# An LSTM decoder on one core: the doubled cell in a PSUM bank, the half cell behind h, and a new spread of two PE jobs

## The chip, the core and the metric

The kernel runs on one core of a Trainium2 chip. Time is device time in microseconds (us) of one launch on that core; smaller is better. The core's engines are TensorE (PE, with its weight loads as PEld), VectorE (DVE), ScalarE (ACT), GpSimd (POOL) and SyncE (SP). They run their own instruction streams and meet through semaphores. PE writes PSUM (eight banks of 128 partitions); DVE and ACT read and write both PSUM and SBUF.

## What is computed

Sixteen sequences of 1024 tokens with 64 features go through three layers with residuals. The second layer is an LSTM autoencoder: two encoder LSTMs (forward, backward) of 1024 steps, then a decoder LSTM of 1024 steps whose input is the same at every step, then a projection. The third is a mixture of 8 experts with the two best chosen per token.

```python
def step(carry, xw):
    h, c = carry
    z = xw + h @ U
    i, f, g, o = jnp.split(z, 4, axis=-1)
    i = jax.nn.sigmoid(i)
    f = jax.nn.sigmoid(f)
    g = jnp.tanh(g)
    o = jax.nn.sigmoid(o)
    c = f * c + i * g
    h = o * jnp.tanh(c)
    return ((h, c), h)
...
h = _L0_tok_ref(x, ...)
h = h + _L0_attn_ref(_layernorm(h, axis=-1), ...)
h = h + _L0_ffn_ref(_layernorm(h, axis=-1), ...)
```

## The kernel before, in words

The program has four parts, one after the other: a set-up, the token mixing, the encoder (both directions interleaved, 1024 steps each), and the decoder, which carries the experts' work in its gaps. The change touches the decoder alone.

**One decoder step.** State lies as 128 hidden units by 16 sequences. PE (`pe_gates`, L733 to 746) multiplies h by U. h is held as two f16 parts, so there are twelve small matmuls: eight on the high part (L740, low then high weights), four on the low part (L743). ACT (`act_gates`) takes the tanh of the gates i, f, g (L751, 48 columns) and of o (L753); the sigmoids are made from tanh of half the argument. DVE (`dve_terms`, L766) makes both products, `dve_sum` (L772) adds them to `twice_cell`, twice the new cell. ACT (`act_cell`, L758) writes tanh of half of that to `tanh_cell`, the first 16 columns of PSUM bank 3. DVE makes the output gate (L789) and the half of twice_cell, the cell that the next step's terms read (`dve_half_cell`, L783), then h: its high part (L797), its full f32 value (L798), and the low part (L803), which waits for L798's semaphore. With the high and the low part PE starts the next step.

DVE's own stream in a step, written in `body` of its block (before, L1349 to 1359): terms, sum, output gate, half cell, the `in_tanh` pieces of the experts' work, then h high, h, h low, then the `in_gates` pieces. All engines work their streams in the order written.

**Bodies and places.** The 1024 steps are 32 bodies of 32 steps (`BODY`). A place is the number of a step in its body, 0 to 31. From body 1 on, each body also carries the experts' work on a tile of 512 tokens: place s carries the tile's part s, and part s + 32 of the tile before. PE's stream at a place is: the twelve gate matmuls, the refill of the input term (`fill`, L1044) at the places that are 1, 3 or 5 in their group of eight, the parts (`pe_part`), then unread products (`pe_idle`, L731: an identity times a constant tile into a spare part of a bank, read by nobody), and at places 7, 15, 23 and 31 one more refill. Their number per place is `idle_products(step, tiles)`: 10 or 13 at places 3 to 18, a small table elsewhere, 5 at place 19.

**The transposes of the experts' sums.** Parts 37 and 38, which fall on places 5 and 6 of the next body, turn the 64 x 512 f32 result `yT` (made by ACT in part 36) in four matmuls (L1129) of one block each, two in each part; the trace records each as two f32 passes. DVE adds them to the residual in part 43, place 11 (L1307). The refill at place 5 stands ahead of them.

So at place s, PE's parts and unread products stand between the gates of step s and the gates of step s + 1. If they take too long, it is h of step s that finds PE busy, and h of step s + 1 that comes late.

Of the kernel before, what the change touches and what calls it, by code (L numbers as in the profile page):

```python
# [6 lines left out]
F32, F16, BF16 = mybir.dt.float32, mybir.dt.float16, mybir.dt.bfloat16  # L7
ALU = mybir.AluOpType
ACT = mybir.ActivationFunctionType
AX = mybir.AxisListType  # L10

P = 128
B, T, D = 16, 1024, 64
# [46 lines left out]
class Links:  # L60


    def __init__(self, engine, sem, base=0):
        self.engine, self.sem, self.base, self.n = engine, sem, base, 0
# [637 lines left out]
class Chain:  # L702
# [3 lines left out]

    def __init__(self, sb, sem, d, name, cell_bank):
        self.d = d  # L710
        self.tanh_cell = cell_bank[:, 0:B]
        self.ifg_cell = sb(f"ifg_cell_{name}", [P, 4, B], F32)
        self.terms = sb(f"terms_{name}", [P, 2, B], F32)
        self.twice_cell, self.tanh_o, self.out_gate, self.h = (
            sb(f"{part}_{name}", [P, B], F32) for part in ("twice_cell", "tanh_o", "out_gate", "h"))
        (self.s_z_ifg, self.s_z_o, self.s_t_ifg, self.s_t_o, self.s_terms, self.s_out_gate, self.s_twice,
         self.s_cell, self.s_tanh_cell, self.s_hi, self.s_h, self.s_lo) = (sem(f"{s}_{name}") for s in (
             "z_ifg", "z_o", "t_ifg", "t_o", "terms", "out_gate", "twice", "cell", "tanh_cell", "hi", "h", "lo"))

    def start(self, nc, own):  # L720

        own.link(nc.vector.memset(self.twice_cell[:], 0.0))
        nc.vector.memset(self.ifg_cell[:, 3, :], 0.0).then_inc(self.s_cell, 1)


# [29 lines left out]

def act_cell(nc, act, c, n):
    act.wait_ge(c.s_twice, n + 1)
    nc.scalar.activation(c.tanh_cell, c.twice_cell[:], ACT.Tanh, scale=0.5).then_inc(c.s_tanh_cell, 1)  # L758


def dve_terms(nc, dve, c, n, own_cell=True):
# [7 lines left out]

def dve_sum(nc, dve, c, n):  # L770
    dve.wait_ge(c.s_terms, n + 1)
    nc.vector.tensor_tensor(c.twice_cell[:], c.terms[:, 0, :], c.terms[:, 1, :], ALU.add).then_inc(c.s_twice, 1)  # L772


def act_out_gate(nc, act, c, n, half_scale):
# [4 lines left out]

def dve_half_cell(nc, dve, c, sums):
    dve.wait_ge(c.s_twice, sums)
    nc.vector.tensor_scalar(c.ifg_cell[:, 3, :], c.twice_cell[:], 0.5, None, ALU.mult).then_inc(c.s_cell, 1)  # L783


def dve_rest(nc, dve, c, n, sums):

    dve.wait_ge(c.s_t_o, n + 1)
    nc.vector.tensor_scalar(c.out_gate[:], c.tanh_o[:], 1.0, 0.5 * X_SCALE, ALU.add, ALU.mult  # L789
                            ).then_inc(c.s_out_gate, 1)  # L790
    dve_half_cell(nc, dve, c, sums)


def dve_hidden(nc, dve, c, n, h_hi):

    tt = nc.vector.tensor_tensor
    tt(h_hi, c.out_gate[:], c.tanh_cell, ALU.mult).then_inc(c.s_hi, 1)  # L797
    tt(c.h[:], c.out_gate[:], c.tanh_cell, ALU.mult).then_inc(c.s_h, 1)  # L798


def dve_hidden_low(nc, dve, c, n, h_hi, h_lo):
    dve.wait_ge(c.s_h, n + 1)
    nc.vector.tensor_tensor(h_lo, c.h[:], h_hi, ALU.subtract).then_inc(c.s_lo, 1)  # L803
# [108 lines left out]
def idle_products(step, tiles):  # L912

    if not tiles or 3 <= step < 19:
        return 10 if step % 2 else 13
    by_place = {0: 0, 1: 4, 2: 5, 19: 5, 20: 9}
    return by_place.get(step, 4 if step % 2 == 0 else 6 if step % STEPS == STEPS - 1 else 5)


QS = BODY * B // P  # L920
# [4 lines left out]
def decoder_and_experts(nc, m):  # L925
# [5 lines left out]

    ctx, sb, sem = tools(nc)
    with ctx:
        c = Chain(sb, sem, 2, "dec", m.bank[3])

        ring_hi = sb("ring_hi", [P, 2, QS, LANES, B], F16)
        ring_lo = sb("ring_lo", [P, 2, QS, LANES, B], F16)
# [70 lines left out]
        with nc.Block() as block:  # L1008
# [29 lines left out]
            def _(pe):  # L1038
# [22 lines left out]
                def pe_part(j, s):  # L1061
# [53 lines left out]
                    if 21 <= s < 20 + 2 * E:  # L1115
# [5 lines left out]
                        elif e + 2 < E:  # L1121
                            pre_x(j, e + 2)
                            pre_mask(j, e + 2)
                    if s in (37, 38):

                        if s == 37:
                            pe.wait_ge(s_yT, j + 1)
                        for blk in range(2 * (s - 37), 2 * (s - 37) + 2):
                            last = mm(pre_bank[0][:, blk * D:(blk + 1) * D], yT[:, blk * P:(blk + 1) * P],  # L1129
                                      m.ident[0:D, 0:D], start=(blk == 0), stop=True, skip_group_check=True)  # L1130
                        if s == 38:
                            last.then_inc(s_yt, 1)

                z = m.bank[4][:, 0:4 * B]
# [72 lines left out]
            def _(dve):  # L1207
# [139 lines left out]
                def body(i, tiles):  # L1347
                    tiles = [(j, start, Own(dve, s_own, DVE_OWN * j)) for j, start in tiles]
                    for step in range(BODY):  # L1349
                        n = BODY * i + step  # L1350
                        dve_terms(nc, dve, c, n)
                        dve_sum(nc, dve, c, n)
                        dve_rest(nc, dve, c, n, n + 1)
                        part(in_tanh, tiles, step)
                        dve.wait_ge(c.s_tanh_cell, n + 1)
                        dve.wait_ge(c.s_out_gate, n + 1)
                        dve_hidden(nc, dve, c, n, h_at(ring_hi, n))
                        dve_hidden_low(nc, dve, c, n, h_at(ring_hi, n), h_at(ring_lo, n))
                        part(in_gates, tiles, step)

# [29 lines left out]
```

## Time and profile before

| | us |
|---|---|
| median of 3 runs | 3947.42 |
| lowest, highest | 3943.25, 3950.13 |
| the profiled execution, its time | 3942.37 |
| its span, first to last instruction | 3940.6 |
| of it: up to the first h of the decoder | 2166.9 |
| of it: first to last h of the decoder | 1736.5 |
| of it: tail behind the last h | 37.2 |

The profile is one execution. A row of the timeline gives the start in us, the length, the engine, the line, the operation, what is written and read, how many alike in a row, and in brackets the engine's idle time ahead with what ended it. In this program start-to-start distances are the safest measure, since matmuls overlap. Between the first and the last h of the decoder lie 1023 steps, 1.697 us each.

### The profile page before, as it was taken

The page shows a single profiled execution, that of the slowest core. Times are in us where ns is not written, and L with a number is a line of the kernel's source. Part 1 is how long each engine was busy: PE and PEld are TensorE (multiplying, and loading weights), DVE is VectorE, ACT ScalarE, POOL GpSimd, SP SyncE. Part 2 cuts the span into 40 slices and gives each one's busy share as a digit, 9 for nine tenths or more (in the row PEclk, how much of TensorE's full clock was granted, in tenths as well). Part 3 has the DMA queues.
Part 4 walks back from the last instruction along what each step waited for, and adds up shares of the span by engine and source line. Part 5 has one row for each costly group of instructions (what it writes and reads, how often), then busy time and mean ns, then how long its engine had stood idle before and what let it go on. Part 6 is the DMA issues. An engine that isn't in the chain of part 4 may idle for free. (4 is left out here: it accounts for less than half of the span.)

```text
span 3940.6 us, 159991 instructions
## 1 busy us (share of the span) xinstructions
PE 3751.8 (95%) x61932; PEld 2744.1 (70%) x61932; DVE 3135.7 (80%) x21227; ACT 2391.8 (61%) x11882; POOL 85.2 (2%) x129
## 2 busy tenths in 40 slices
PE   6899899999999999999999899999999999999998
PEld 3233688888888888888888666666666666666664
DVE  5888899999999999999998677667776667776675
ACT  3223688888888888888888334444434444444443
POOL 6100000000000000000000000000000000000000
PEclk8999999999999999999999999999999999999999
DMA  3010000000000000000000000000000000000000
GB/s 90 18 26 20 8 3 3 3 3 3 3 3 3 3 3 3 3 3 3 3 3 5 4 8 8 6 6 8 8 8 6 8 6 8 8 8 6 6 8 7
DMA packets 49571, 34.01 MB, mean 9 GB/s; under 512 B 37661, under 2 KB 46877, under 8 KB 48806
## 3 DMA queue, kind: packets, MB, share of 16 engines
q1 hardware_dynamic: 48806, 23.77, 2.3%
q8 instruction: 485, 7.95, 0.8%
q14 instruction: 280, 2.29, 0.2%
HBM read 15.37 MB, written 8.39 MB: 6 GB/s over the span
## 5 line engine op out<-in xcount | busy, mean ns | idle before, releaser
L731 PE MATMUL bank<-xs,ident 128*128 128x128 f16 x15583 | 1413.9, 222 | 0.0
L731 PEld LDWEIGHTS bank<-xs,ident 128*128 128x128 f16 x15583 | 1010.1, 102 | 252.3 <-issue 230.0
L751 ACT ACTIVATE ifg_cell_dec<-bank 128x48 f32<-128x48 f32 x1024 | 215.1, 210 | 640.4 <-PE bank L743 640.4
L743 PE MATMUL bank<-enc_lo,u_hi 128*128 128x16 f16 x8192 | 528.9, 173 | 0.3 <-DVE enc_lo L803 0.3
L740 PE MATMUL bank<-enc_hi,u_lo 128*128 128x16 f16 x8192 | 527.2, 172 | 0.0
L766 DVE SCALAR_TENSOR_TENSOR terms_dec<-ifg_cell_dec 128x32 f32<-128x32 f32 x1024 | 196.7, 192 | 397.9 <-ACT ifg_cell_dec L751 386.7
L740 PE MATMUL bank<-enc_hi,u_hi 128*128 128x16 f16 x8192 | 500.5, 169 | 0.0
L740 PEld LDWEIGHTS bank<-enc_hi,u_lo 128*128 128x128 f16 x8192 | 338.8, 96 | 206.4 <-DVE enc_hi L797 171.9
L758 ACT ACTIVATE bank<-twice_cell_dec 128x16 f32<-128x16 f32 x1024 | 191.7, 187 | 402.2 <-DVE twice_cell_dec L772 402.2
L743 PEld LDWEIGHTS bank<-enc_lo,u_hi 128*128 128x128 f16 x8192 | 338.6, 96 | 67.8 <-DVE enc_lo L803 0.4
L740 PE MATMUL bank<-ring_hi,u_lo 128*128 128x16 f16 x4096 | 260.4, 172 | 102.0 <-DVE ring_hi L797 95.5
L740 PEld LDWEIGHTS bank<-enc_hi,u_hi 128*128 128x128 f16 x8192 | 349.7, 96 | 0.0
L777 ACT ACTIVATE out_gate_bwd<-tanh_o_bwd,encoder_half_scale 128x16 f32<-128x16 f32 x1024 | 315.2, 308 | 33.6
L777 ACT ACTIVATE out_gate_fwd<-tanh_o_fwd,encoder_half_scale 128x16 f32<-128x16 f32 x1024 | 315.1, 308 | 33.5
L843 PE MATMUL bank<-xs,w_lo 128*128 128x128 f16 x1024 | 322.3, 315 | 0.0
L845 PE MATMUL bank<-ones,bias 128*128 128x128 bf16 x1024 | 322.3, 315 | 0.0
L740 PEld LDWEIGHTS bank<-ring_hi,u_lo 128*128 128x128 f16 x4096 | 183.7, 97 | 180.5 <-DVE ring_hi L797 159.6
L841 PE MATMUL bank<-xs,w_hi 128*128 128x128 f16 x1024 | 277.2, 271 | 1.4 <-PEq L432 1.4
L743 PE MATMUL bank<-ring_lo,u_hi 128*128 128x16 f16 x4096 | 263.0, 172 | 0.7 <-DVE ring_lo L803 0.5
L740 PE MATMUL bank<-ring_hi,u_hi 128*128 128x16 f16 x4096 | 250.3, 169 | 0.0
L1119 PE MATMUL bank<-hid,w 128*64 128x512 f32 x448 | 240.1, 618 | 0.0
L758 ACT ACTIVATE bank<-twice_cell_bwd 128x16 f32<-128x16 f32 x1025 | 192.0, 187 | 54.2
(268 smaller groups left out, 7889.5 us busy)
## 6 DMA issues: line engine op xcount, KB each, us to landing
g_rows<-tok_d_gamma_batched_dram SPq DMA_DIRECT2D x8, 512.0 KB, 6.5
x_rows<-in_x_dram SPq DMA_DIRECT2D x16, 256.0 KB, 3.1
kept_h<-tok_ln_h SPq DMA_DIRECT2D x32, 128.0 KB, 2.1
res<-kept_h SPq DMA_DIRECT2D x32, 128.0 KB
out_dram<-sums SPq DMA_DIRECT2D x32, 128.0 KB
raw_wd<-in_L_attn_Wd_dram SPq DMA_DIRECT2D x2, 256.0 KB
raw_experts<-in_L_ffn_W_dram SPq DMA_DIRECT2D x2, 256.0 KB
raw_u<-in_L_attn_Uf_dram SPq DMA_DIRECT2D x1, 256.0 KB
```

The lines of the kernel that those rows point to most:

```text
L731: nc.tensor.matmul(spare, m.ident16[:], m.xs[:, 0, :, :].rearrange("p b t -> p (b t)"), start=False, stop=True, skip_group_check=True)
L740: nc.tensor.matmul(z[k], w[:, g, :], h_hi, start=False, stop=False, skip_group_check=True)
L743: last = nc.tensor.matmul(z[k], m.u_hi[c.d][:, g, :], h_lo, start=False, stop=True, skip_group_check=True)
L751: nc.scalar.activation(c.ifg_cell[:, 0:3, :], ifg, ACT.Tanh, scale=1.0 / Z_SCALE).then_inc(c.s_t_ifg, 1)
L758: nc.scalar.activation(c.tanh_cell, c.twice_cell[:], ACT.Tanh, scale=0.5).then_inc(c.s_tanh_cell, 1)
L766: nc.vector.scalar_tensor_tensor(c.terms[:], c.ifg_cell[:, 0:2, :], 1.0, c.ifg_cell[:, 2:4, :], ALU.add, ALU.mult).then_inc(c.s_terms, 1)
L777: nc.scalar.activation(c.out_gate[:], c.tanh_o[:], ACT.Identity, scale=0.5 * X_SCALE, bias=half_scale).then_inc(c.s_out_gate, 1)
L841: nc.tensor.matmul(z, m.w_hi[d][:, g, :], x, start=(k in (0, 3)), stop=False, skip_group_check=True)
L843: nc.tensor.matmul(z, m.w_lo[d][:, g, :], x, start=False, stop=False, skip_group_check=True)
L845: nc.tensor.matmul(z, m.lstm_bias[d][:, GATE_FROM[g], :], m.ones3[:].rearrange("p (b t) -> p b t", b=B), start=False, stop=False, skip_gro ...
L1119: mm(y_bank[0:D, :], m.w2[:, e, :], hid[:, e % 2, :], start=False, stop=False, skip_group_check=True)
```

## The change

It does four things, all in the decoder.

- `twice_cell` of the decoder moves from SBUF to columns 16 to 31 of PSUM bank 3, beside `tanh_cell`. The sum (L773 after) writes PSUM; ACT's tanh of the cell (L759 after) and the half cell (L784 after) read PSUM. The encoder's two chains keep theirs in SBUF.
- The decoder's half cell goes from ahead of h (and of the `in_tanh` pieces) to between the f32 h (L798) and the low part (L803).
- The four transposes go one to a place, at places 5, 6, 7 and 8 instead of two at 5 and two at 6; the semaphore that tells DVE of them is raised at place 8 instead of 6.
- Place 19 has 2 unread products instead of 5.

```diff
-    def __init__(self, sb, sem, d, name, cell_bank):
+    def __init__(self, sb, sem, d, name, cell_bank, twice_in_bank=False):
...
         self.tanh_cell = cell_bank[:, 0:B]
+        self.twice_cell = cell_bank[:, B:2 * B] if twice_in_bank else sb(f"twice_cell_{name}", [P, B], F32)[:]
...
-def dve_rest(nc, dve, c, n, sums):
+def dve_out_gate(nc, dve, c, n):
 
     dve.wait_ge(c.s_t_o, n + 1)
     nc.vector.tensor_scalar(c.out_gate[:], c.tanh_o[:], 1.0, 0.5 * X_SCALE, ALU.add, ALU.mult
                             ).then_inc(c.s_out_gate, 1)
-    dve_half_cell(nc, dve, c, sums)
...
-    by_place = {0: 0, 1: 4, 2: 5, 19: 5, 20: 9}
+    by_place = {0: 0, 1: 4, 2: 5, 19: 2, 20: 9}
...
-        c = Chain(sb, sem, 2, "dec", m.bank[3])
+        c = Chain(sb, sem, 2, "dec", m.bank[3], twice_in_bank=True)
...
-                    if s in (37, 38):
+                    if 37 <= s < 37 + QS:
...
-                        for blk in range(2 * (s - 37), 2 * (s - 37) + 2):
-                            last = mm(pre_bank[0][:, blk * D:(blk + 1) * D], yT[:, blk * P:(blk + 1) * P],
-                                      m.ident[0:D, 0:D], start=(blk == 0), stop=True, skip_group_check=True)
-                        if s == 38:
+                        blk = s - 37
+                        last = mm(pre_bank[0][:, blk * D:(blk + 1) * D], yT[:, blk * P:(blk + 1) * P],
+                                  m.ident[0:D, 0:D], start=(blk == 0), stop=True, skip_group_check=True)
+                        if blk == QS - 1:
                             last.then_inc(s_yt, 1)
...
                         dve_sum(nc, dve, c, n)
-                        dve_rest(nc, dve, c, n, n + 1)
+                        dve_out_gate(nc, dve, c, n)
                         part(in_tanh, tiles, step)
...
                         dve_hidden(nc, dve, c, n, h_at(ring_hi, n))
+                        dve_half_cell(nc, dve, c, n + 1)
                         dve_hidden_low(nc, dve, c, n, h_at(ring_hi, n), h_at(ring_lo, n))
```

DVE's stream of one step (place 6 of a body, with one `in_tanh` piece, L1328), before:

```order
L772 TENSOR_TENSOR twice_cell_dec<-terms_dec 128x16 [waits terms_dec]
L789 TENSOR_SCALAR out_gate_dec<-tanh_o_dec 128x16 [waits t_o_dec]
L783 TENSOR_SCALAR ifg_cell_dec<-twice_cell_dec 128x16 [waits twice_dec]
L1328 TENSOR_SCALAR half_bits<-var 128x4 [waits ff_dve_step]
L797 TENSOR_TENSOR ring_hi<-out_gate_dec,bank 128x16 [waits out_gate_dec,tanh_cell_dec]
```

and after:

```order
L773 TENSOR_TENSOR bank<-terms_dec 128x16 [waits terms_dec]
L790 TENSOR_SCALAR out_gate_dec<-tanh_o_dec 128x16 [waits t_o_dec]
L1328 TENSOR_SCALAR half_bits<-var 128x4 [waits ff_dve_step]
L797 TENSOR_TENSOR ring_hi<-out_gate_dec,bank 128x16 [waits out_gate_dec,tanh_cell_dec]
L798 TENSOR_TENSOR h_dec<-out_gate_dec,bank 128x16
L784 TENSOR_SCALAR ifg_cell_dec<-bank 128x16 [waits twice_dec]
```

The sum now writes the bank, and the half cell (L783, now L784) stands behind h (L798) instead of ahead of the high part (L797).

PE's stream from the transposes of place 5 to the end of place 7, before:

```order
L1129 MATMUL bank<-ident,ff_yT 128x64 [waits yT_kept]
L1129 MATMUL bank<-ident,ff_yT 128x64
L731 MATMUL bank<-xs,ident 128x128 x10
L740 MATMUL bank<-ring_hi,u_lo 128x16 [waits hi_dec]
L740 MATMUL bank<-ring_hi,u_lo 128x16 x3
L740 MATMUL bank<-ring_hi,u_hi 128x16 x4
L743 MATMUL bank<-ring_lo,u_hi 128x16 [waits lo_dec]
L743 MATMUL bank<-ring_lo,u_hi 128x16 x3
L1129 MATMUL bank<-ident,ff_yT 128x64 x2
L731 MATMUL bank<-xs,ident 128x128 x13
```

and after, from the one of place 6 to the products of place 7:

```order
L1129 MATMUL bank<-ident,ff_yT 128x64
L732 MATMUL bank<-xs,ident 128x128 x13
L741 MATMUL bank<-ring_hi,u_lo 128x16 [waits hi_dec]
L741 MATMUL bank<-ring_hi,u_lo 128x16 x3
L741 MATMUL bank<-ring_hi,u_hi 128x16 x4
L744 MATMUL bank<-ring_lo,u_hi 128x16 [waits lo_dec]
L744 MATMUL bank<-ring_lo,u_hi 128x16 x3
L1129 MATMUL bank<-ident,ff_yT 128x64
L732 MATMUL bank<-xs,ident 128x128 x10
```

One transpose stands at each of places 5, 6, 7 and 8; the unread products of these places keep their numbers.

## Rows read from the trace of the kernel before

**Rows 1.** The profile's page: busy us (share of the span) and instructions, by engine.

```profile
PE 3751.8 (95%) x61932; PEld 2744.1 (70%) x61932; DVE 3135.7 (80%) x21227; ACT 2391.8 (61%) x11882; POOL 85.2 (2%) x129
```

**Rows 2.** Timeline, one decoder step, behind place 7 of body 14.

```profile
2938.72 0.19 ACT L758 ACTIVATE bank<-twice_cell_dec 128x16 f32<-128x16 f32 x1 [0.39 <-DVE twice_cell_dec L772]
...
2938.94 0.17 DVE L797 TENSOR_TENSOR ring_hi<-out_gate_dec,bank 128x16 f16<-128x16 f32 x1
2939.03 0.17 DVE L798 TENSOR_TENSOR h_dec<-out_gate_dec,bank 128x16 f32<-128x16 f32 x1
...
2939.17 0.26 PE L740 MATMUL bank<-ring_hi,u_lo 128*128 128x16 f16 x4 [0.39 <-DVE ring_hi L797]
2939.22 0.18 DVE L803 TENSOR_TENSOR ring_lo<-h_dec,ring_hi 128x16 f16<-128x16 f32 x1
...
2939.46 0.26 PE L743 MATMUL bank<-ring_lo,u_hi 128*128 128x16 f16 x4
...
2939.73 0.21 ACT L751 ACTIVATE ifg_cell_dec<-bank 128x48 f32<-128x48 f32 x1 [0.82 <-PE bank L743]
...
2939.97 0.19 DVE L766 SCALAR_TENSOR_TENSOR terms_dec<-ifg_cell_dec 128x32 f32<-128x32 f32 x1
```

**Rows 3.** Four answers on stretches, their sums: h 22-23, 5-6, 6-7, 19-20, 31 each.

```profile
sum 52.21, PE 52.21; mean PE 1.68
...
sum 53.22, PE 53.06; mean PE 1.71
...
sum 58.65, PE 54.92; mean PE 1.77
...
sum 54.34, PE 54.32; mean PE 1.75
```

**Rows 4.** Two stretches h 6-7: start:end, us, PE busy, PEclk, DMA share, GB/s.

```profile
2339.28:2341.61 2.33, 2.33 (x34) 0.50 0.03 7
...
2937.24:2938.94 1.70, 1.53 (x35) 1.00 0.03 10
```

**Rows 5.** Timeline of PE, place 6 of body 14 and the next gates.

```profile
2936.26 0.66 PE L1129 MATMUL bank<-ident,ff_yT 64*128 64x64 f32 x4
2936.85 0.90 PE L731 MATMUL bank<-xs,ident 128*128 128x128 f16 x13
2937.58 0.25 PE L740 MATMUL bank<-ring_hi,u_lo 128*128 128x16 f16 x4
```

**Rows 6.** Timeline, body 14: h and low-part gates behind place 2 and behind place 19.

```profile
2930.47 0.17 DVE L797 TENSOR_TENSOR ring_hi<-out_gate_dec,bank 128x16 f16<-128x16 f32 x1
...
2930.98 0.26 PE L743 MATMUL bank<-ring_lo,u_hi 128*128 128x16 f16 x4
...
2959.16 0.17 DVE L797 TENSOR_TENSOR ring_hi<-out_gate_dec,bank 128x16 f16<-128x16 f32 x1
...
2959.76 0.24 PE L743 MATMUL bank<-ring_lo,u_hi 128*128 128x16 f16 x4
```

**Rows 7.** Lines of ACT: ns min/median/max of one, first and last start, shapes.

```profile
L751 ACT ACTIVATE ifg_cell_dec<-bank x1024: 210/210/213, 2165.9 to 3902.5; 128x48 f32<-128x48 f32 x171
...
L275 ACT COPY bv<-bv x1: 193/193/193, 16.2 to 16.2; 64x3 f32<-64x3 f32 x1
...
L1181 ACT COPY ff_h_kept<-ff_h x32: 387/388/408, 2242.7 to 3913.4; 128x256 f32<-128x256 f32 x32
...
L758 ACT ACTIVATE bank<-twice_cell_dec x1024: 187/187/189, 2166.7 to 3903.2; 128x16 f32<-128x16 f32 x171
```

**Rows 8.** Lines of DVE: one that reads PSUM, one that reads SBUF alone.

```profile
L797 DVE TENSOR_TENSOR ring_hi<-out_gate_dec,bank x1024: 170/172/173, 2166.9 to 3903.4; 128x16 f16<-128x16 f32 x171
...
L803 DVE TENSOR_TENSOR ring_lo<-h_dec,ring_hi x1024: 174/175/178, 2167.2 to 3903.7; 128x16 f16<-128x16 f32 x171
```

**Rows 9.** Timeline of DVE in the encoder: h, terms (L766), low part of h.

```profile
1500.17 0.16 DVE L798 TENSOR_TENSOR h_bwd<-out_gate_bwd,bank 128x16 f32<-128x16 f32 x1
...
1500.38 0.17 DVE L803 TENSOR_TENSOR enc_lo<-h_bwd,enc_hi 128x16 f16<-128x16 f32 x1
```

More of the change, by code:

```diff
@@ L702 @@
 class Chain:
-    def __init__(self, sb, sem, d, name, cell_bank):
+    def __init__(self, sb, sem, d, name, cell_bank, twice_in_bank=False):
         self.d = d
         self.tanh_cell = cell_bank[:, 0:B]
+        self.twice_cell = cell_bank[:, B:2 * B] if twice_in_bank else sb(f"twice_cell_{name}", [P, B], F32)[:]
         self.ifg_cell = sb(f"ifg_cell_{name}", [P, 4, B], F32)
         self.terms = sb(f"terms_{name}", [P, 2, B], F32)
-        self.twice_cell, self.tanh_o, self.out_gate, self.h = (
-            sb(f"{part}_{name}", [P, B], F32) for part in ("twice_cell", "tanh_o", "out_gate", "h"))
+        self.tanh_o, self.out_gate, self.h = (
+            sb(f"{part}_{name}", [P, B], F32) for part in ("tanh_o", "out_gate", "h"))
         (self.s_z_ifg, self.s_z_o, self.s_t_ifg, self.s_t_o, self.s_terms, self.s_out_gate, self.s_twice,
@@ L720, in start @@
     def start(self, nc, own):
-        own.link(nc.vector.memset(self.twice_cell[:], 0.0))
+        own.link(nc.vector.memset(self.twice_cell, 0.0))
         nc.vector.memset(self.ifg_cell[:, 3, :], 0.0).then_inc(self.s_cell, 1)
@@ L757, in act_cell @@
     act.wait_ge(c.s_twice, n + 1)
-    nc.scalar.activation(c.tanh_cell, c.twice_cell[:], ACT.Tanh, scale=0.5).then_inc(c.s_tanh_cell, 1)
+    nc.scalar.activation(c.tanh_cell, c.twice_cell, ACT.Tanh, scale=0.5).then_inc(c.s_tanh_cell, 1)
 def dve_terms(nc, dve, c, n, own_cell=True):
@@ L771, in dve_sum @@
     dve.wait_ge(c.s_terms, n + 1)
-    nc.vector.tensor_tensor(c.twice_cell[:], c.terms[:, 0, :], c.terms[:, 1, :], ALU.add).then_inc(c.s_twice, 1)
+    nc.vector.tensor_tensor(c.twice_cell, c.terms[:, 0, :], c.terms[:, 1, :], ALU.add).then_inc(c.s_twice, 1)
 def act_out_gate(nc, act, c, n, half_scale):
@@ L782, in dve_half_cell @@
     dve.wait_ge(c.s_twice, sums)
-    nc.vector.tensor_scalar(c.ifg_cell[:, 3, :], c.twice_cell[:], 0.5, None, ALU.mult).then_inc(c.s_cell, 1)
-def dve_rest(nc, dve, c, n, sums):
+    nc.vector.tensor_scalar(c.ifg_cell[:, 3, :], c.twice_cell, 0.5, None, ALU.mult).then_inc(c.s_cell, 1)
+def dve_out_gate(nc, dve, c, n):
     dve.wait_ge(c.s_t_o, n + 1)
```

## The prediction, written before the result was known

> **What bounds the kernel now.** I read the busy shares first [rows 1]: PE is busy for 95% of the span. That says nothing here, because PE runs unread products in every gap. The change lies between the first and the last h of the decoder, 1736.5 us, so I read the timeline of one step there [rows 2]. It is a loop through four hand-overs: ACT's tanh of the cell at 2938.72, h high at 2938.94 (0.22 later), h at 2939.03, h low at 2939.22, the gates on it at 2939.46, ACT's gates at 2939.73, DVE's terms at 2939.97, then the sum, and the next tanh of the cell. PE sits idle for 0.39 us ahead of its gates there, so PE is not the bound of this step; the loop of latencies is.
>
> Then I measured the time from h to h by place, over the 31 bodies that carry a tile [rows 3]. Place 23 is an ordinary one: 52.21 / 31 = 1.684 us. Nearly all places stand there. Three don't. The step behind place 5 sums to 53.22 (1.01 over the ordinary), behind place 6 to 58.65 (6.44 over), behind place 19 to 54.34 (2.13 over). So the decoder has a floor of 1.684 us a step and some 9.6 us above it at just the places that the change edits.
>
> Why those: behind place 19, h is at 2959.16 and the gates on its low part start at 2959.76, 0.60 later [rows 6], against 0.52 in the free step [rows 2]: PE was still at its parts and products. Places 5 and 6 hold two transposes each. Behind place 6 the 31 stretches are of two kinds: 21 of about 1.70 us at full granted clock, and ten of 2.2 to 2.4 us at a granted clock of 0.50, that is the lower level of 1.2 GHz, one of each in [rows 4]. What PE did before the clock fell is the same in all ten: the transposes of places 5 and 6, with the products pushed late behind them.
>
> **The change, part by part.**
>
> Place 19: a product costs (2937.58 - 2936.85) / 13 = 0.056 us [rows 5]. Three fewer give PE 0.17 us back where it is 0.08 late [rows 6]. The excess goes whole: **-2.1 us**, and 0.09 of slack stays for a shorter loop.
>
> Transposes: two take 2936.85 - 2936.26 = 0.59, one 0.295 us [rows 5]. One fewer at places 5 and 6 takes 0.295 off a PE that is late by 0.03 at most: that part of the excess goes. One more at places 7 and 8 is hidden as long as PE idles there longer: behind place 7 the row says 0.39 idle [rows 2], and place 8 is like it; 0.1 stays. The reader of the sums is at place 11, three places behind the last transpose, and waits no longer. The falls of the clock cost ten times 0.62 = 6.2 us. I expect them to stop: in any stretch over places 5 and 6 PE now has half the transposes, and the products of both places start 0.3 us sooner. Transposes: **-7.5 us** (6.44 + 1.01). If only the lateness went and the clock still fell, it would be -1.3.
>
> Tanh of the cell: ACT's L758 takes 187 ns, SBUF in and PSUM out. What is the input worth? SBUF to SBUF is 193 ns at 3 columns and 388 at 256 [rows 7]: 0.77 ns a column, 203 at 16. PSUM to SBUF is 210 at 48 columns, so 185 at 16. The difference, 18 to 20 ns, is what reading PSUM saves; ACT starts behind a wait in all of them. h follows ACT's end and not DVE's half cell (0.22 behind the start of both, also where a further DVE instruction stands between), so all of it reaches the path. I take 20 ns; were the last columns cheaper than the slope says, up to 25.
>
> The sum's write: no row has DVE writing PSUM. From below: ACT's output in PSUM instead of SBUF is 203 - 187 = 16 ns shorter. From above: no row gives it directly; the largest step that any row shows between the two memories is the same 20 to 25 ns, taken with the other sign. In between lie DVE's own rows, nearest to it: it reads PSUM in 172 ns and SBUF alone in 175 [rows 8], no difference worth a price. I take 0, ends -16 and +25.
>
> The half cell: it leaves the place ahead of h, where it cost nothing (h waits for ACT), and comes between h and its low part. h low waits 0.19 to 0.20 us for h anyway [rows 2]. In the encoder an instruction of double width stands at this very spot, and the low part starts 0.21 behind h [rows 9], with 16 columns more, some 17 ns at DVE's pace; narrower it would be 0.20, so 0 to +10 ns a step; I take 0. Its reader, the next terms, starts 0.75 us later [rows 2], so nobody waits for the cell. What queues behind it on DVE is only h low and the experts' pieces.
>
> ScalarE and VectorE have prices on a page too. The Trainium skill, "VectorE: DVE Perf Modes", section on the TRN2 errata, gives ScalarE 224 cycles for an SBUF source and 172 for a PSUM one, which would be 43 ns, and VectorE 58 and 120, which would be 65 ns more for a PSUM source. The trace agrees in sign for ACT at less than half the size, and not for DVE, whose PSUM-reading row is 3 ns shorter. By the page's ACT figure alone the cell's term would be some 44 us instead of 20.
>
> Sum of the cell: 1024 x 20 ns = 20.5. PE takes some back: behind place 2 the low-part gates are 0.51 behind h [rows 6], straight behind the high-part ones, so PE has no slack at all, and two more places (23 and 31, with a refill behind their products) look alike in the timeline. Three places x 31 x about 15 ns = 1.4. **-19 us.**
>
> Together -2.1 - 7.5 - 19 = -28.6. The profiled execution took 3942.37, so 3913.8; it lay 5 us below the median of 3947.4, which gives 3918.8. I say **3918 us**.
>
> **The rivals.**
>
> Rival 1, the write eats the cell's gain: DVE's sum ends 20 to 25 ns later in PSUM, or the half cell delays h low by 10 and the write by 10. For it: no row shows that write. Against: DVE's reads show no cost. The time is 3947 - 9.6 + 0 to 5 = 3938 to 3943.
>
> Rival 2, the clock still falls, at places 5 and 6 (a transpose is still in each) or newly at place 19, which loses three products. For it: the fall follows the work that PE got, and the number of falls hangs on how bodies lie in time. Against: none of 31 bodies fell at 19, where matmuls of 256 and 512 columns surround it. The time is 3918 + 6 = 3924.
>
> Rival 3, **slower**: a DVE instruction that touches the bank costs a hand-over more, twice on the path, once when the sum is written and once when the half cell reads in front of h low. A hand-over is 35 ns (ACT's end at 2938.91 to h at 2938.94 [rows 2]), so +70 - 20 = +50 ns a step, 51 us, less 9.6: 3989 us. It wins over the rest from 30 ns a step on. Against it: L797 and L798 both touch the bank and follow each other by 0.09. The Trainium skill, "Perfetto Trace Analysis", section "Optimizing Scalar/DVE Operations", has this mechanism as a rule: about 60 ns of access for DVE on SBUF and 125 on PSUM. By that rule, the trace disagrees for reads.
>
> Rival 4, the shorter loop uncovers PE at more places than the three: most places from 21 on run their products up to the gates. Were it a dozen places that give back a third of the 20 ns each, it is 12 x 31 x 7 ns = 2.6 us, inside the range.
>
> **How the numbers follow.** Forecast 0.60; rival 1 0.17; rival 2 0.10; rival 3 0.09; rest 0.04, in which the write is cheaper and the time near 3900. The low end: -16 for the write and 25 for ACT, 41 x 1024 less what PE takes back (3) is -39, with -9.6: 3899. The high end takes in rival 1. Range **3898 to 3943**. A measurement of this kernel can tell about 0.2%, 8 us: faster needs under 3939.5. Forecast, rival 2, the rest and a third of rival 1 lie there: faster 0.79, same 0.12, slower 0.09.
>
> **What would show it.** L759 at 162 to 169 ns, L773 near 174 ns, h 0.19 to 0.20 behind the start of L759, h low still 0.20 behind h; the stretch of place 23 near 1.666 us; behind places 5, 6 and 19 the same as there, no granted clock of 0.50 in the 31 stretches of place 6; places 7 and 8 with PE idle of 0.1. Wrong would be an L773 of 195 ns or more, or h low 0.21 or more behind h.

## The result, and the profile after

The changed kernel takes 3930.27 us (median of 5, 3927.74 to 3930.87) against 3947.42 (median of 5, 3943.25 to 3950.13): 17 us less, a ratio of 0.9956 with a 95% interval of 0.9943 to 0.9969. The interval leaves out 1: the change is faster, by 0.44%. The forecast was 3918. About three fifths of the forecast gain came.

The profiled execution took 3930.27 us, its span is 3928.5. The step loop first. Timeline of the changed kernel around h behind place 6 of body 14, as [rows 2] (which is behind place 7; both are free steps); columns: start us, length us, engine, line, operation, out<-in, shapes, how many, idle ahead:

```profile
2932.73 0.17 ACT L759 ACTIVATE bank<-bank 128x16 f32<-128x16 f32 x1 [0.40 <-DVE bank L773]
...
2932.93 0.17 DVE L797 TENSOR_TENSOR ring_hi<-out_gate_dec,bank 128x16 f16<-128x16 f32 x1
2933.02 0.16 DVE L798 TENSOR_TENSOR h_dec<-out_gate_dec,bank 128x16 f32<-128x16 f32 x1
2933.10 0.17 DVE L784 TENSOR_SCALAR ifg_cell_dec<-bank 128x16 f32<-128x16 f32 x1
...
2933.22 0.18 DVE L803 TENSOR_TENSOR ring_lo<-h_dec,ring_hi 128x16 f16<-128x16 f32 x1
...
2933.45 0.26 PE L744 MATMUL bank<-ring_lo,u_hi 128*128 128x16 f16 x4
...
2933.72 0.21 ACT L752 ACTIVATE ifg_cell_dec<-bank 128x48 f32<-128x48 f32 x1 [0.82 <-PE bank L744]
```

h is 0.20 behind the start of the tanh, where it was 0.22. The half cell (L784) now sits between h and its low part, and the low part is still 0.20 behind h.

The two lines that changed, as [rows 7] (ns min/median/max of one; first and last start):

```profile
L773 DVE TENSOR_TENSOR bank<-terms_dec x1024: 182/182/185, 2169.6 to 3890.3; 128x16 f32<-128x16 f32 x171
...
L759 ACT ACTIVATE bank<-bank x1024: 168/168/168, 2169.8 to 3890.6; 128x16 f32<-128x16 f32 x171
```

The tanh went from 187 to 168 ns. The sum's write went to 182; in the same execution the same line in the encoder, writing SBUF, takes:

```profile
L773 DVE TENSOR_TENSOR twice_cell_fwd<-terms_fwd x1024: 174/174/177, 427.4 to 2162.8; 128x16 f32<-128x16 f32 x171
```

A tanh 19 ns shorter and a sum 8 ns longer: the ordinary step has a median of 1.675 us instead of 1.684 (the start of h high follows the start of the tanh by 200 ns instead of 219, the tanh follows the start of the sum by 217 instead of 208). 9 ns x 1023 = 9.2 us. In the changed kernel the median is 1.675 or 1.676 us at every place.

The stretches, as [rows 3], sums of 31 for h 5-6, 6-7 and 19-20 of the changed kernel:

```profile
sum 51.99, PE 51.64; mean PE 1.67
...
sum 52.27, PE 51.88; mean PE 1.67
...
sum 52.13, PE 51.90; mean PE 1.67
```

They were 53.22, 58.65 and 54.34. An ordinary place of the changed kernel (h 10-11, below) sums to 51.87, so all three have come down to the floor but for single odd steps:

```profile
sum 51.87, PE 44.84; mean PE 1.45
```

Of the ten stretches h 6-7 at a granted clock of 0.50 one is left (as [rows 4]: start:end, us, PE busy, PEclk, DMA share, GB/s):

```profile
3685.83:3687.67 1.84, 1.84 (x24) 0.50 0.00 0
```

It is longer than those of before: the next stretch, h 7-8, is at 0.50 too, and so is h 8-9 (2.43 us as well), so this one fall costs 1.7 us.

```profile
3687.67:3690.10 2.43, 2.43 (x30) 0.50 0.03 7
```

And the decoder from its first to its last h (engines' busy us with counts, PEclk, DMA), 1720.78 us against 1736.50:

```profile
2169.97:3890.75 1720.78, 1638.98 (x24847) 1135.20 (x24845) 1133.47 (x8276) 675.47 (x3471) 0.00 (x0) 1.00 0.03 7
```

What lies ahead of the decoder took 3.1 us longer in this execution than in the one of before (first h at 2169.97 against 2166.87), with the same instructions; over the executions of this study the first h came at 2166.9 to 2176.3. So the decoder's own stretch, first to last h, is what the experiments are compared by, beside their times.

### The profile page after: what moved, and what is told of

The parts are those of the page before. It is cut to its first block and busy times, and to the rows that moved or that the text cites. A ratio compares the mean times of both kernels' runs of the same rounds, so it can differ in the third digit from the quotient of the medians.

```text
span 3928.5 us, 159805 instructions
## 1 busy us (share of the span) xinstructions
PE 3759.6 (96%) x61839; PEld 2742.2 (70%) x61839; DVE 3055.2 (78%) x21227; ACT 2369.2 (60%) x11882; POOL 85.8 (2%) x129
## 5 line engine op out<-in xcount | busy, mean ns | idle before, releaser
L732 PE MATMUL bank<-xs,ident 128*128 128x128 f16 x15490 | 1399.2, 221 | 0.0
L732 PEld LDWEIGHTS bank<-xs,ident 128*128 128x128 f16 x15490 | 995.8, 101 | 256.4 <-issue 230.0
L759 ACT ACTIVATE bank<-bank 128x16 f32<-128x16 f32 x1024 | 172.0, 168 | 411.5 <-DVE bank L773 411.5
L797 DVE TENSOR_TENSOR ring_hi<-out_gate_dec,bank 128x16 f16<-128x16 f32 x1024 | 174.7, 171 | 147.6 <-ACT bank L759 133.1
```

The costliest lines, as they stand in the source:

```text
L732: nc.tensor.matmul(spare, m.ident16[:], m.xs[:, 0, :, :].rearrange("p b t -> p (b t)"), start=False, stop=True, skip_group_check=True)
L759: nc.scalar.activation(c.tanh_cell, c.twice_cell, ACT.Tanh, scale=0.5).then_inc(c.s_tanh_cell, 1)
```

## The experiments

The comparisons in time are each with the kernel before on the same chip. D is the stretch from the first to the last h of the decoder in the profiled execution. A "fall" is a time at which the granted clock went to 0.50 behind places 5 to 8. In every kernel the clock is also at 0.50 around the decoder's first h and once more in the first steps of body 1; these two are not counted.

| run | ratio to before, 95% | D, us | ordinary step, ns | falls |
|---|---|---|---|---|
| before | 1 | 1736.5 | 1684 | 10 |
| changed kernel | 0.9956 (0.9943 to 0.9969) | 1720.8 | 1675 | 1 |
| cell alone (e1) | 0.9981 (0.9973 to 0.9990) | 1729.3 | 1675 | 10 |
| PE alone (e2) | 0.9988 (0.9980 to 0.9997) | 1730.8 | 1684 | 4 |
| half cell moved (e3) | 1.0003 (0.9994 to 1.0012) | 1735.4 | 1684 | 6 |
| transposes alone (e5) | 0.9993 (0.9983 to 1.0002) | 1735.2 | 1684 | 6 |
| place 19 alone (e6) | 0.9996 (0.9986 to 1.0005) | 1741.4 | 1684 | 20 |
| encoder's cells too (e7) | 0.9957 (0.9943 to 0.9970) | 1718.9 | 1675 | 0 |
| h in PSUM too (e8) | 0.9987 (0.9977 to 0.9996) | 1729.3 | 1683 | 2 |
| products first (e9) | 0.9984 (0.9975 to 0.9993) | 1731.1 | 1684 | 0 |
| changed, products first (e10) | 0.9957 (0.9944 to 0.9971) | 1719.3 | 1675 | 0 |
| changed again (e11) | 0.9955 (0.9942 to 0.9967) | 1719.3 | 1675 | 0 |
| PE alone, products first (e12) | 0.9977 (0.9968 to 0.9987) | 1726.8 | 1683 | 0 |

### The cell's half alone

```diff
-        c = Chain(sb, sem, 2, "dec", m.bank[3])
+        c = Chain(sb, sem, 2, "dec", m.bank[3], twice_in_bank=True)
...
-                        dve_rest(nc, dve, c, n, n + 1)
+                        dve_out_gate(nc, dve, c, n)
...
+                        dve_half_cell(nc, dve, c, n + 1)
```

> The kernel before with the cell's half of the change alone: the decoder's doubled cell in PSUM bank 3, the half cell behind h; the transposes and place 19 as before. Theory A (the loop of latencies sets a step, -19 ns for the tanh, +8 for the sum's write, as the changed kernel's rows say): the ordinary decoder step is 1.675 us instead of 1.684, the steps behind places 5, 6 and 19 keep PE's time, so 29 of 32 places gain 9 ns: -8.6 us, 3939 against 3947, and the granted clock still falls to 0.50 behind place 6 in some ten bodies. Rival B (PE's work takes back what the loop gives wherever products run up to the gates, so that the two halves of the change need each other): places 21 to 31 stay at 1.684 and the gain is 5 us or less.

Measured: 3936.14 us against 3943.64, -7.5 us; D -7.2. The ordinary step is 1.675 us at places 21 to 31 too, so PE takes nothing back there: rival B is out. The gain is below 9.2 us because the steps behind places 5, 6 and 19 keep PE's time, and for one more reason, which stands at the half cell's move. Behind places 6 and 19 PE's time stays, and the falls stay (sum of the 31 stretches h 6-7, and of h 19-20):

```profile
sum 58.93, PE 55.26; mean PE 1.78
...
sum 54.15, PE 54.15; mean PE 1.75
```

### PE's half alone

```diff
-    by_place = {0: 0, 1: 4, 2: 5, 19: 5, 20: 9}
+    by_place = {0: 0, 1: 4, 2: 5, 19: 2, 20: 9}
...
-                    if s in (37, 38):
+                    if 37 <= s < 37 + QS:
...
```

> The kernel before with PE's half of the change alone: one transpose to a place, 2 unread products at place 19; the cell stays in SBUF. Theory A: the steps behind places 5, 6 and 19 come down to 1.684 us like the rest, no or one fall of the granted clock in the 31 bodies: -9.6 us less what a fall costs, 3938 to 3940. Rival B (the shorter loop was needed to keep the clock up, since the products crowd together more): the clock still falls in several bodies behind places 5 to 8 and the gain is 3 to 5 us.

Measured: 3938.45 us, -5.2 us; D -5.7. The lateness went as expected (ordinary steps of 1.684 us behind 5, 6 and 19), but four falls stayed, two of them here (stretches h 6-7; fields as [rows 4]):

```profile
2825.30:2827.42 2.12, 2.12 (x27) 0.50 0.00 0
2934.38:2936.38 2.00, 2.00 (x26) 0.50 0.00 0
```

Theory A had the steps right, rival B the falls and, nearly, the gain (3 to 5 us). A fall costs more here than in the kernel before, since it runs on into place 7: 1.0 us instead of some 0.6. The two halves add to 12.9 us of D where the whole change gives 15.7, and the falls are most of the rest: four of them cost 4.0 us here, the one of the changed kernel 1.7. Whether rival B's cause, the longer step, is right too is taken up behind the last experiment on the clock.

### The half cell's move alone

```diff
-    dve_half_cell(nc, dve, c, sums)
...
                         dve_hidden(nc, dve, c, n, h_at(ring_hi, n))
+                        dve_half_cell(nc, dve, c, n + 1)
```

> The kernel before with one edit: the half cell behind h instead of ahead of it, doubled cell still in SBUF. Theory A (h waits for ACT, h low waits for h's semaphore, the half cell fits in both gaps): h stays 219 ns behind the start of the tanh, h low 198 ns behind h, the step 1.684 us, the time within 2 us of before. Rival C (the half cell ahead of h held it by some ns, so that a part of the 19 ns belongs to the move): h 5 ns or more earlier, up to -5 us. Rival D (it holds h low): h low up to 10 ns later, up to +10 us.

Measured: 3944.69 us against 3943.64, the interval holds 1; the ordinary step is 1.684. Timeline of DVE, high part, h, half cell, low part:

```profile
2939.23 0.17 DVE L796 TENSOR_TENSOR ring_hi<-out_gate_dec,bank 128x16 f16<-128x16 f32 x1
2939.32 0.16 DVE L797 TENSOR_TENSOR h_dec<-out_gate_dec,bank 128x16 f32<-128x16 f32 x1
2939.40 0.17 DVE L783 TENSOR_SCALAR ifg_cell_dec<-twice_cell_dec 128x16 f32<-128x16 f32 x1
2939.52 0.18 DVE L802 TENSOR_TENSOR ring_lo<-h_dec,ring_hi 128x16 f16<-128x16 f32 x1
```

The low part stays 0.20 behind h with the half cell in between. In an ordinary step the move is free in both directions, C and D are out, and the 9 ns a step belong to the bank. The half cell here reads SBUF and takes 168 ns; the one of the changed kernel reads PSUM and takes 167.

The move isn't quite free over the whole decoder. Bodies 1 to 31, without places 5 to 8 and 19, hold single steps that are more than 40 ns longer than the ordinary one. All six traces with the half cell ahead of h have 18 of them, 3.2 us over in sum; all seven with it behind h have 23, 4.4 to 4.7 us. What makes these steps long isn't shown.

### One PE edit at a time

Transposes one to a place, place 19 with 5 products:

```diff
-                    if s in (37, 38):
+                    if 37 <= s < 37 + QS:
...
```

> The kernel before with one edit: one transpose to a place at 5, 6, 7, 8. Theory A: the steps behind places 5 and 6 come down to 1.684 us, the step behind 19 stays at 1.75, at most one or two falls of the clock behind places 5 to 8: -7.5 us, 3940. Rival B (the falls only move to places 7 and 8): the sums of the steps behind 7 and 8 grow by several us and the gain is 1 to 3 us.

Measured: 3943.44 us against 3945.76, not clear of no change; D -1.3. The step behind place 5 came down (median 1.684 from 1.717), the step behind 19 stayed at 1.75, but the profiled execution had six falls. They still begin around h of place 6 but now run on through place 7. Sums of 31 stretches, h 6-7 and h 7-8:

```profile
sum 54.31, PE 53.92; mean PE 1.74
...
sum 56.35, PE 55.83; mean PE 1.80
```

An ordinary 31 are 52.21, so the six falls cost 2.1 + 4.1 = 6.2 us, 1.0 each. The ten of before cost about as much, at some 0.6 each. So of the 7.5 us only the lateness came, the 1.3 us of D. That is rival B: a small gain, and the step behind place 7 grown by several us (place 8 is as before).

Place 19 with 2 products, transposes as before:

```diff
-    by_place = {0: 0, 1: 4, 2: 5, 19: 5, 20: 9}
+    by_place = {0: 0, 1: 4, 2: 5, 19: 2, 20: 9}
```

> The kernel before with one edit: 2 unread products at place 19 instead of 5. Theory A: the step behind place 19 comes down from 1.746 to 1.684 us in each of 31 bodies, -1.9 us, at the edge of what can be timed; no fall of the clock near places 19 to 21. Rival F (the clock falls there for want of products): steps of 2.2 us at half clock at places 19 to 22 in some bodies, +3 to +6 us.

Measured: 3941.23 us against 3945.76, interval 0.9986 to 1.0005, so the time alone does not tell it. The trace does. Sums of 31 stretches, h 19-20 and h 6-7:

```profile
sum 52.52, PE 52.34; mean PE 1.69
...
sum 65.28, PE 63.20; mean PE 2.04
```

The step behind 19 is down by 1.8 us, as expected, and no fall lies near it: F is out. The second sum is the surprise. Nothing at places 5 and 6 was edited, and this one execution had 20 falls there where the one of before had 10; its time was 3950.46, 9 us over the median of its kernel. Its ten executions fall into two groups: eight at a mean granted clock of 0.986 to 0.988, 3940 to 3944 us, as the kernel before has them, and two at 0.981, 3950 us, one of them the profiled one. None of the 31 executions of before on this chip lay under 0.983. So the number of falls changes from execution to execution of one program; whether this edit makes the bad executions more frequent, two of ten can't tell.

### Is 8 ns the price of a DVE write into PSUM?

```diff
-        self.tanh_o, self.out_gate, self.h = (
-            sb(f"{part}_{name}", [P, B], F32) for part in ("tanh_o", "out_gate", "h"))
...
+        self.h = cell_bank[:, 2 * B:3 * B] if twice_in_bank else sb(f"h_{name}", [P, B], F32)
```

> The changed kernel with the decoder's f32 h in PSUM bank 3 too: L798 then writes PSUM and L803 reads it. It asks whether the 8 ns of the sum's write are a price of any DVE write into PSUM. Theory A: L798 takes 164 + 8 = 172 ns, h low starts 206 ns behind h instead of 198, the decoder step is 1.683 us, +8 us, 3938. Rival G (the sum's 8 ns come from its two SBUF inputs with a PSUM output; an instruction that reads PSUM and writes PSUM pays nothing): h low stays 198 behind h and the step 1.675.

Measured: the ordinary step is 1.683 us, D is 1729.3 (+8.5 over the changed kernel), the ratio 0.9987. The same line of the program with an SBUF and with a PSUM output, and the low part that now reads PSUM:

```profile
L799 DVE TENSOR_TENSOR h_fwd<-out_gate_fwd,bank x1024: 162/164/166, 429.5 to 2163.4; 128x16 f32<-128x16 f32 x171
L799 DVE TENSOR_TENSOR bank<-out_gate_dec,bank x1024: 172/172/179, 2170.2 to 3899.5; 128x16 f32<-128x16 f32 x171
...
L804 DVE TENSOR_TENSOR ring_lo<-bank,ring_hi x1024: 162/174/176, 2170.4 to 3899.7; 128x16 f16<-128x16 f32 x171
```

The low part starts 206 ns behind h instead of 198. Theory A holds to the nanosecond: 8 ns for writing there, nothing for reading from there (174 against 175 in [rows 8]). G is out. The write costs 8 ns with two SBUF inputs (the sum) and with one SBUF and one PSUM input (h).

### What makes the clock fall

```diff
+                        ahead = bool(tiles) and step in (5, 6)
+                        if ahead:
+                            pe_idle(nc, m, m.bank[1 - q % 2][:, HALF - P:], idle_products(step, tiles))
                         for j, start in tiles:
                             pe_part(j, start + step)
-                        pe_idle(nc, m, m.bank[1 - q % 2][:, HALF - P:], idle_products(step, tiles))
+                        if not ahead:
+                            pe_idle(nc, m, m.bank[1 - q % 2][:, HALF - P:], idle_products(step, tiles))
```

> The kernel before with one edit: at places 5 and 6 PE's unread products stand ahead of the two transposes instead of behind them; the numbers of both stay. It asks what makes the granted clock fall there. Theory H (what counts is that the products come late behind the transposes, so that PE has a stretch of small matmuls and transposes with few products in it): no or one or two falls, the stretches behind place 6 at 1.70 to 1.72, -5 to -6 us. Rival I (two places with two f32 transposes each are too little work in either order): some ten falls remain and the time is that of before.

Measured: 3938.85 us against 3945.76, -6.9 us, ratio 0.9984; D -5.4. No fall, with two transposes at both places and PE late as before. Its timeline of PE at places 5 and 6, and the sum of the stretches h 6-7, 53.43 where it was 58.65:

```profile
2936.04 0.72 PE L731 MATMUL bank<-xs,ident 128*128 128x128 f16 x10
2936.69 0.66 PE L1129 MATMUL bank<-ident,ff_yT 64*128 64x64 f32 x4
2937.28 0.26 PE L740 MATMUL bank<-ring_hi,u_lo 128*128 128x16 f16 x4
...
2937.60 0.89 PE L731 MATMUL bank<-xs,ident 128*128 128x128 f16 x13
2938.41 0.66 PE L1129 MATMUL bank<-ident,ff_yT 64*128 64x64 f32 x4
```

```profile
sum 53.43, PE 47.83; mean PE 1.54
```

Theory H holds and rival I is out: with the same transposes and products at these two places, and PE without a gap in either order (in body 14 of both traces PE has no idle time from the gates of place 5 to those behind place 6), it is the order that makes the clock fall. With the products behind, gates, a refill, two transposes and, after ten products, gates and two transposes again followed each other. One profile without a fall could be chance, but the mean granted clock of all executions says the same: 0.990 or 0.991 in all ten, where the 31 of before on this chip stand at 0.983 to 0.990. The order alone is worth as much as the whole of PE's half.

To see whether this closes the gap of PE's half, the order was put on top of it:

```diff
+                        ahead = bool(tiles) and 5 <= step <= 8
+                        if ahead:
+                            pe_idle(nc, m, m.bank[1 - q % 2][:, HALF - P:], idle_products(step, tiles))
...
```

> PE's half of the change alone (one transpose to a place, 2 unread products at place 19, cell in SBUF) with the products ahead of the transpose at places 5 to 8. With the products behind them this half left five falls. Theory H: no falls, steps of 1.684 us everywhere, first to last h 1727 us against 1730.8; -9 us against before (0.9977). Rival K (five falls came from the slower loop alone, whatever the order): several falls remain and the time is that of PE's half as it was, 0.9988.

Measured: 0.9977, D 1726.8, no fall, as theory H says in all three numbers; K is out. (The trace of PE's half has four falls behind these places, not the five of the expectation.) D is 9.7 below before, and that is the 9.6 that the prediction put on these edits.

### The changed kernel again, and with the products first

> The changed kernel itself, to stand beside the next two on one chip. Theory A: decoder step 1.675 us, none to two falls of the granted clock to 0.50 in the 31 bodies, 17 us (0.44%) less than before; its executions spread over 3 to 4 us where those of before spread over 7 to 11, because the number of falls changes from execution to execution in before.

Measured: 3933.75 us against 3949.37 (0.9955), no fall, D 1719.3. Its five executions spread over 7 us this time, not 3 to 4, so that part was wrong: with all five at a granted clock of 0.990 or 0.991, their spread doesn't come from falls.

The same with the edit above:

> The changed kernel with PE's unread products ahead of the transpose at places 5 to 8. Theory H (the products behind the transposes make the clock fall): no fall at all in the 31 bodies, the steps behind places 5 to 8 at 1.675 us; 0 to 2 us less than the changed kernel, since it had one fall left, of 1.7 us. Rival J (at places 7 and 8 the transpose, now last, meets h, which PE's table had free): the steps behind 7 and 8 come out longer than 1.675 us, up to +2 us.

Measured: 3934.39 us, the same as its neighbour within the intervals; no fall; the four places at 1.675 us, sum of the stretches h 6-7:

```profile
sum 52.15, PE 51.09; mean PE 1.65
```

J is out. With the fall or none that the changed kernel has, there is nothing left to gain.

Does the shorter step itself help the clock? The mean granted clock of every execution is on record, and the profiled ones show what it stands for: 0.990 or 0.991 with no fall or one, 0.989 with two, 0.987 or 0.988 with four or six, 0.986 or 0.987 with ten, 0.981 with twenty.

| kernel | transposes a place | products | step, ns | executions | mean granted clock, lowest to highest |
|---|---|---|---|---|---|
| before | 2 | behind | 1684 | 72 | 0.983 to 0.990 |
| cell alone (e1) | 2 | behind | 1675 | 11 | 0.982 to 0.988 |
| PE alone (e2) | 1 | behind | 1684 | 11 | 0.985 to 0.990 |
| transposes alone (e5) | 1 | behind | 1684 | 10 | 0.987 to 0.991 |
| h in PSUM too (e8) | 1 | behind | 1683 | 10 | 0.987 to 0.990 |
| changed kernel, both times | 1 | behind | 1675 | 10 | 0.990 to 0.991 |
| products first (e9) | 2 | ahead | 1684 | 10 | 0.990 to 0.991 |
| PE alone, products first (e12) | 1 | ahead | 1683 | 10 | 0.990 to 0.991 |

It helps, but only together with the spread. e8 is the changed kernel with the same work in the same order on PE and a step 8 ns longer, and the falls come back. The shorter step without the spread (e1) changes nothing. So rival B of PE's half was right in its cause as well, as long as the products stand behind the transposes; with the products ahead the step's length doesn't matter (e12). Why 8 or 9 ns a step decide it isn't shown.

### The encoder's cells in PSUM too

```diff
-        self.twice_cell = cell_bank[:, B:2 * B] if twice_in_bank else sb(f"twice_cell_{name}", [P, B], F32)[:]
+        self.twice_cell = cell_bank[:, B:2 * B]
...
-                        dve_half_cell(nc, dve, ch[d], n + 1 + d)
+                        dve_copy(nc, ch[d])
+                        dve_half_of_copy(nc, dve, ch[d], n)
```

> The changed kernel with the encoder's doubled cells in PSUM too (banks 6 and 7). There the half cell would read the bank while ACT does, so DVE makes the sum twice, first into PSUM for the tanh, then into SBUF, and halves the second one; both stand in the gap in which DVE waits for the tanh. Theory A (the encoder's loop runs through sum, tanh, h, terms of the other direction; each of its 2048 half-steps, 0.845 us now, loses 19 ns and gains 8): 10 ns x 2048 = 20 us less than the changed kernel, 3910. Rival E (the second sum and the half cell run into h, 0.42 us behind the sum, or ACT's output gate becomes the bound): 0.845 us stays or grows, 3930 or more.

Measured: 3926.66 us against 3943.64, 0.9957, just the changed kernel's ratio. The 20 us didn't come. The tanh did shorten there (h 0.20 behind its start), but the half-step is 0.84 to 0.85 us as before. Timeline of DVE, a half-step:

```profile
1500.10 0.19 DVE L769 SCALAR_TENSOR_TENSOR terms_bwd<-ifg_cell_bwd 128x32 f32<-128x32 f32 x1
1500.20 0.17 DVE L814 TENSOR_TENSOR enc_lo<-h_fwd,enc_hi 128x16 f16<-128x16 f32 x1
...
1500.94 0.19 DVE L769 SCALAR_TENSOR_TENSOR terms_fwd<-ifg_cell_fwd 128x32 f32<-128x32 f32 x1
```

and ACT's gates ahead of those terms, with PE's gates on the low part:

```profile
1500.70 0.21 ACT L754 ACTIVATE ifg_cell_fwd<-bank 128x48 f32<-128x48 f32 x1
```

```profile
1500.43 0.26 PE L746 MATMUL bank<-enc_lo,u_hi 128*128 128x16 f16 x4
```

The encoder's loop runs past the tanh of the cell: terms of one direction (1500.10), behind them in DVE's order the low part of the other's h (1500.20), PE's gates (1500.43), ACT's (1500.70), the terms of that direction (1500.94). 0.10 + 0.23 + 0.27 + 0.24 = 0.84. The tanh and the sum are on the other, shorter way round. It is not much shorter: in the kernel before, the low part starts 0.213 us behind h in the median, where the decoder's, which waits for h alone, needs 0.198. In e7 it is 0.223 to 0.225, so the 10 ns that the tanh's way gained went into that wait. The expectation read the encoder's loop as the decoder's, and theory A failed there. Rival E said that the half-step stays, and it did, though for neither of E's two causes.

## Why the prediction was right or wrong

**The bound.** The loop of hand-overs sets a decoder step, PE's share of 95% says nothing: right. Each hand-over but the two that were edited kept its length to the nanosecond or two, and the gain of the ordinary step is the 19 ns of the tanh less the 8 or 9 of the write.

**Place 19, -2.1.** Right: 1.8 us alone in e6, and the median step went from 1.746 to 1.675 in the changed kernel, 9 ns of that the loop's.

**Transposes, -7.5.** Of this, 1.3 was lateness, and that part is right (e5). The other 6.2 was the falls, and there the number came for a reason that the prediction didn't give. It had them stop because half the transposes stand in a stretch and the products start 0.3 us sooner. That is e5 and e2, and they still had six and four falls, each dearer than before, and e5 gained none of the 6.2. In the changed kernel they are gone but for one because its step is 9 ns shorter as well, which the prediction didn't count on; to that extent it is luck. What it named as common to all falls, the products behind the transposes, is the cause that the experiments bear out: turned round, the order leaves no fall in the profiles of e9 and e12, and a granted clock of 0.990 or 0.991 in all twenty of their executions. At places 7 and 8 PE is not late, as forecast (its gates start 0.23 us behind h), though the record shows no idle PE there, and not 0.1.

**Tanh of the cell, 20 ns.** Measured 19. The way there, SBUF to SBUF against PSUM to SBUF from rows of other shapes, came out right. It passed over a row of the kernel before that has the second at the very width, 178 ns where the slope gave 185 (fields: busy us, mean ns of one, idle us):

```profile
L753 ACT ACTIVATE tanh_o_dec<-bank 128x16 f32<-128x16 f32 x1024 | 182.4, 178 | 0.0
```

Against it the changed kernel's tanh, PSUM to PSUM in 168, also tells what ACT's output is worth: 10 ns less into PSUM than into SBUF, where DVE pays 8 ns more.

**The sum's write, taken as 0 between -16 and +25.** This is the term that was mis-sized: it is +8. The value was taken from DVE's reads, as the nearest rows of that engine. A read's price says nothing here on a write's: e8 has a write at +8 and a read at -1 side by side. ACT's sign, taken as the bound from below, is the opposite of DVE's. With 8 the cell's term is (20 - 8) x 1024 = 12 instead of 20 us.

**The half cell, 0.** Right for the ordinary step, in e3 and in the trace; the low part starts 198 ns behind h with or without it. Over the decoder the move costs some 1.3 us in single long steps, a term that the prediction doesn't have.

**PE takes 1.4 us back at places 2, 23 and 31.** Wrong, it takes nothing: their median step is 1.675 us in the changed kernel and in e1. That the low-part gates stood straight behind the high-part ones, 0.51 behind h, was no sign of PE being the bound.

The sum with what was measured: -9.2 for the loop, -9.7 for PE's edits (e12), 18.9 us in the profiled decoder. 17.2 were seen in e11 (1736.5 - 1719.3), and the single long steps are most of the difference; 15.7 in the first profile, which had the fall of 1.7. In the medians of the whole kernel it is 15.6 (e11) and 17.2 us (first result). What is missing to the forecast of 28.6 is the cell's term, forecast at 19 and measured at 9 a decoder, less those steps.

**The rivals.** Rival 1 (the write eats the cell's gain) is the one that came in part: 8 of 19 ns. Rival 2 (the clock still falls) came for one fall in one profile, and for several wherever the step stayed long and the products behind the transposes. Rival 3 (a dearer DVE access to the bank, twice) is out: the write costs 8 ns, and the reads of h low and of the half cell cost nothing. Its hand-over of 35 ns is a little too long as well; it is 32 in the medians (219 behind the tanh's start, less the 187 that it takes).

Rival 3's rule of the Trainium skill, "Perfetto Trace Analysis", section "Optimizing Scalar/DVE Operations", puts DVE's access at about 60 ns on SBUF and 125 on PSUM, a difference of 65. The trace agrees in direction for a DVE write, at 8 ns, and not for its reads, where it shows no difference (168 against 167 for the half cell). The Trainium skill, "VectorE: DVE Perf Modes", section on the TRN2 errata, puts ScalarE's PSUM source 52 cycles under its SBUF source, by the prediction's estimate 43 ns; the trace has 19.

## What to carry to other kernels

In a loop of latencies, price each hand-over by engine, by memory and by direction, and treat a write and a read as different things: here a tensor that ACT reads and DVE writes won 19 ns at one end and lost 8 at the other. Before a gain is claimed for a second loop, follow that loop's own circle in the timeline; an instruction of the same kind can lie off it. Where filler work keeps PE's clock up, try it ahead of slow small matmuls before you thin them out: here that alone stopped the falls. Judge by several executions, and by the granted clock of each, since the number of falls in one profile changes from execution to execution, and count what a fall costs as well as how many there are.

## What the runs showed of the hardware that was not expected

- A 128x16 f32 instruction of DVE takes 8 ns longer with its output in PSUM (174 to 182 for the sum, 164 to 172 for h), and no longer with an input there (175 to 174 for the low part, 168 to 167 for the half cell). ACT's 128x16 tanh from PSUM takes 168 ns into PSUM (L759 after) and 178 into SBUF (L753 before).
- The granted clock fell or not at the same amount of PE work in the same two steps, by its order alone: ten falls in the profile with the transposes first, none with the products first, and 0.990 or 0.991 as the mean of all ten executions.
- With one transpose a place, the products behind it, a step 8 ns longer brought falls back: 0.987 to 0.990 in ten executions (e8) against 0.990 to 0.991 in ten of the changed kernel.
- The number of falls in the one profiled execution of kernels with the same work at places 5 and 6 was 10, 10, 6 and 20 (before, e1, e3, e6).
